# Low and high parts side by side in one 512-wide product, their sum formed by three engines

## The chip, the cores and the metric

One Trainium2 chip, of which the kernel uses one core. The metric is the device time of one execution in microseconds (us). TensorE does the matrix products, VectorE, ScalarE and GpSimd the rest, SyncE issues most DMAs. Each engine works through a queue of its own in order; semaphores hold one queue until another has got far enough.

## The reference, cut to what matters

Eight graphs of C = 1024 nodes with D = 256 features, hidden width 512. With H = (adj != 0) as 0/1 numbers, w the first row of adj, Dn = 1/(H w) and Be = 1/(column sums of H):

```
m   = Be * (H^T x)                 (S1)
z   = Dn * (H m)                   (S2)
h   = relu(z W1^T + b1)            (P, M)
q   = layernorm(h) W2^T            (Q)
m   = Be * (H^T q)                 (S3)
y   = Dn * (H m) + b2 + x          (S4)
x1  = layernorm(x + y)
out = layernorm(x1 + relu([x1, adj x1 / deg] WL^T))   (V, VM, L)
```

H holds only 0 and 1. x and m are f32 and are split into a high and a low f32r part, each of which is multiplied by H; the two products are summed.

## The kernel before, in words

Rows of 128 nodes are a tile, so a graph has NT = 8 tiles. For one graph TensorE runs the stages S2, P/M, Q, S3, S4, V/VM, L and then S1 of the next graph, with nothing between them. A bank of PSUM is 512 f32 columns wide; the table PRODUCT_BANKS gives the bank of each tile in each stage, and each stage waits for a bank until the tile that was in it before is emptied.

S1, S3 and S4 compute one output tile of 128x256 as 8 inner steps of two products each, one with the high and one with the low part (x_hi, x_lo, or m_hi, m_lo); both go to columns 0 to 255 of the bank. In S1 the high product is 258 wide: columns of ones behind x_hi count the column sums of H for Be. The helper tiled (L1077) runs S3, S4 and L: the first tiles of a stage (four in S3, two in S4) are filled step by step together, so the stage can start before its last input is there; the others follow one after the other, 8 steps each. Between the first three steps of S3 stand the last three tiles of Q. In front of tile 6 of S4 stand the transposes of tiles 0 and 1 of x1 (L1248), behind S4 the one of tile 2, and then V (L1267, L1268) and VM (L1274) take one tile of x1 at a time, with the transpose three tiles ahead. V waits until TX, the bank of the transpose, is emptied, which is take_x1 on ScalarE (L693, L695) and then x1_low on VectorE (L981).

Behind S1 and S3, ScalarE rounds Be times the bank into m_hi (L561) and VectorE takes the rest as m_lo (L790), which empties the bank. S4 and S2 want one tile of m a step. In S1, VectorE takes Be from the counted column (L832, L835), and between the tiles it builds the next rows of HT (L808).

Between the m_lo of S3, VectorE sums Dn of the next graph over 1024 columns with two inputs in SBUF (L758), in front of tiles 4, 5 and 7 and behind 7. Behind S4, VectorE adds Dn times the bank to the residual xres (L991), takes the moments of the row (L998, L1005), in tiles 2 to 6 builds a tile of H of the next graph (L747), and the reciprocal of the root (L774). ScalarE takes the root (L566), GpSimd two small shifts (L461, L463), ScalarE centres the rows (L687).

GpSimd's queue in a graph: z_cross (L470), the sums of squares (L477), x_lo (L481), the four operations on WL (L488, L493), the shifts with x1_cross (L500), the split of the next x (L432), the shifts of the last norm, and at the end the residual of the next graph: 8 doublings of x (L451) and 8 additions of b2 (L457). In the first graph the b2 additions stand before WL. ScalarE prepares WL_high and WL_cross (L679, L682) behind its last m_hi. SyncE loads x of the next graph when the residual is built, and adj of the next graph from the end of M on.

Of the kernel before, what the change touches and what calls it, by code (L numbers as in the profile page):

```python
# [42 lines left out]
H_EARLY = 5  # L43
X1_IN_H = 6
# [4 lines left out]
def graph_net(nc, x, adj, W1, b1, gamma, beta, W2, b2, WL, out):  # L49
# [80 lines left out]
    with ctx:  # L130
# [16 lines left out]
        x_hi, _, _ = place("x_hi", [P, NT, DP], F32R)  # L147
        x_lo, x_lo_at, _ = place("x_lo", [P, NT, D], F32R)
        m_hi, m_hi_at, _ = place("m_hi", [P, NT, D], F32R)
        m_lo, m_lo_at, _ = place("m_lo", [P, NT, D], F32R)  # L150
# [23 lines left out]
        hT, _, _ = place("hT", [P, NH, C], F32, m_hi_at)  # L174
# [15 lines left out]
        WL_high, _, nxt = place("WL_high", [P, ND, 2 * D], F32R, x_lo_at)  # L190
        WL_low, _, nxt = place("WL_low", [P, ND, 2 * D], F32R, nxt)
        assert nxt <= x_lo_at + 4 * NT * D
        WL_cross = [x_hi[:, 2 * d:2 * d + 2, 0:D] for d in range(ND)]
        x1_high = [x_hi[:, 2 * ND + n, 0:D] for n in range(X1_SLOTS)]
        x1_low, _, nxt = place("x1_low", [P, X1_SLOTS, D], F32R, H_at + 4 * C * X1_IN_H)
        x1_cross, _, nxt = place("x1_cross", [P, X1_SLOTS, D], F32R, nxt)
        assert nxt <= H_at + 4 * C * NT and 2 * ND + X1_SLOTS <= NT

        W1n, _, nxt = place("W1n", [P, NH, D], F32, m_hi_at)
# [6 lines left out]
        assert nxt <= m_lo_at + 4 * NT * D and m_lo_at == m_hi_at + 4 * NT * D  # L206
# [9 lines left out]
        zero_c = small[:, 23, 0:1]  # L216
        stats, _, _ = place("stats", [P, NT, 6], F32)
# [31 lines left out]
        be_done, rBe_ready, m_hi_done = (sem(n) for n in ("be_done", "rBe_ready", "m_hi_done"))  # L249
# [166 lines left out]
        def _(pool):  # L416
# [48 lines left out]
            def graph(b, more, first=False):  # L465
# [24 lines left out]
                for d in range(ND):  # L490
                    pool.wait_ge(WL_scaled, b * ND + d + 1)
                    pool.wait_ge(WL_low_done, b * ND + d + 1)
                    nc.gpsimd.tensor_tensor(WL_cross[d], WL_cross[d].bitcast(F32),  # L493
                                            WL_low[:, d, :].bitcast(F32).rearrange("p (a c) -> p a c", a=2),
# [30 lines left out]
        def _(act):  # L525
# [102 lines left out]
            def graph(b, more):  # L628
# [47 lines left out]
                for e in range(NT):  # L676
                    take_m_hi("S3", e, b, NT + e)
# [643 lines left out]
```

## Time and profile before

| | |
|---|---|
| median of 3 runs | 1051.67 us (1051.66 to 1051.96) |
| profiled execution | 1051.42 us, span 1049.6 us |
| TensorE busy | 1039.2 us of the span |
| VectorE busy | 776.7 us |
| ScalarE busy | 433.3 us |
| GpSimd busy | 435.6 us |

The span runs from the first to the last instruction of the core, the execution's own time is 1.8 us longer. TensorE's matmuls are pipelined: the duration of one in a row is longer than the distance from its start to the next one's start, and the pace is read from a stretch of many. An instruction of another engine that starts right behind one of its own does so some 0.05 to 0.1 us before the recorded end of the first.

### The profile page before, as it was taken

What the parts mean: (1) busy time and instruction counts of PE and PEld (TensorE: products, weight loads), DVE (VectorE), ACT (ScalarE), POOL (GpSimd) and SP (SyncE); (2) the same over time, 40 slices, a digit from 0 to 9 for tenths busy, and PEclk for the clock granted to TensorE, in tenths of its full rate; (3) what the DMA queues carried; (4) which work ended last, traced back from release to release, by engine and by line L of the source; (5) the groups of instructions that cost most, each with busy time, mean ns of one, the idle gap of its engine ahead of it and who ended that gap; (6) DMA issues with size and microseconds to landing.
All of it is one profiled execution on the core that took longest, in us unless ns stands there. A gap on an engine that the chain in (4) does not pass through costs nothing.

```text
span 1049.6 us, 19643 instructions
## 1 busy us (share of the span) xinstructions
PE 1039.2 (99%) x6241; PEld 933.2 (89%) x6241; DVE 776.7 (74%) x1848; ACT 433.3 (41%) x1029; POOL 435.6 (41%) x674
## 2 busy tenths in 40 slices
PE   8999999999999999999999999999999999999997
PEld 8889898898989989899898998989889898888986
DVE  6878786787867878677786778676786777867355
ACT  5553523445234442445325362254622536225350
POOL 0357416434254433534344353543525534265320
PEclk9999999999999999999999999999999999999999
DMA  8065431734227441274414644044440634400001
GB/s 296 3 138 117 98 90 34 152 92 103 64 59 156 96 98 31 60 160 100 90 30 87 133 100 100 20 114 106 100 100 20 142 78 100 110 11 1 2 1 40
DMA packets 72032, 90.01 MB, mean 86 GB/s; under 512 B 15544, under 2 KB 61248, under 8 KB 72000
## 3 DMA queue, kind: packets, MB, share of 16 engines
q1 hardware_dynamic: 63232, 85.49, 35.1%
q10 hardware_dynamic: 8768, 4.10, 1.7%
q8 instruction: 19, 0.31, 0.1%
q14 instruction: 13, 0.11, 0.0%
HBM read 81.14 MB, written 8.42 MB: 85 GB/s over the span
## 4 chain that ended last, share of the span: by engine, by line
PE 99%; DMA 0%; DVE 0%; issue 0%; ACT 0%; DVEq 0%
PE bank L1077 45%; PE bank L1107 12%; PE bank L1183 11%; PE bank L1231 11%; PE bank L1212 3%; PE bank L1219 3%; PE bank L1274 3%; PE bank L1267 3%; PE bank L1268 3%; PE bank L1211 3%; PE bank L1248 1%; PE bank L1068 1%; PE bank L1234 1%; DMA raw<-in_adj_dram 0%; PE bank L1172 0%; DVE xres L779 0%
## 5 line engine op out<-in xcount | busy, mean ns | idle before, releaser
L1077 PE MATMUL bank<-yv,adjT 128*128 128x257 f32 x1024 | 223.3, 379 | 0.0
L1077 PEld LDWEIGHTS bank<-yv,adjT 128*128 128x128 f32 x1024 | 193.6, 189 | 28.7
L566 ACT ACTIVATE small<-mv,small 128x1 f32<-128x1 f32 x192 | 56.0, 291 | 247.8 <-DVE mv L785 144.6
L1077 PE MATMUL bank<-x_hi,H 128*128 128x256 f32 x512 | 125.1, 286 | 0.0
L1231 PE MATMUL bank<-gW2T,hT 128*128 128x257 f32 x512 | 123.7, 385 | 0.0
L1107 PE MATMUL bank<-x_hi,H 128*128 128x258 f32 x512 | 123.6, 289 | 0.0
L1077 PE MATMUL bank<-x_lo,H 128*128 128x256 f32 x512 | 122.4, 280 | 0.0
L1077 PE MATMUL bank<-m_hi,HT 128*128 128x256 f32 x512 | 122.0, 281 | 0.0
L1077 PE MATMUL bank<-m_lo,HT 128*128 128x256 f32 x512 | 121.4, 279 | 0.0
L1107 PE MATMUL bank<-x_lo,H 128*128 128x256 f32 x512 | 119.2, 282 | 0.0
L561 ACT ACTIVATE m_hi<-bank,small 128x256 fp32r<-128x256 f32 x128 | 57.5, 474 | 136.2 <-DVE small L835 75.6
L1231 PEld LDWEIGHTS bank<-gW2T,hT 128*128 128x128 f32 x512 | 93.0, 190 | 11.5
L1183 PE MATMUL bank<-HT,m_lo 128*128 128x512 f32 x256 | 101.8, 398 | 0.0
L1183 PE MATMUL bank<-HT,m_hi 128*128 128x512 f32 x256 | 101.0, 395 | 0.0
L461 POOL TENSOR_TENSOR small<-mv,small 128x1 f32<-128x1 f32 x120 | 30.0, 250 | 170.0 <-DVE small L774 170.0
L1077 PEld LDWEIGHTS bank<-x_hi,H 128*128 128x128 f32 x512 | 96.8, 189 | 0.0
L1077 PEld LDWEIGHTS bank<-x_lo,H 128*128 128x128 f32 x512 | 96.3, 188 | 0.0
L1077 PEld LDWEIGHTS bank<-m_lo,HT 128*128 128x128 f32 x512 | 96.1, 188 | 0.0
L1077 PEld LDWEIGHTS bank<-m_hi,HT 128*128 128x128 f32 x512 | 96.1, 188 | 0.0
L790 DVE SCALAR_TENSOR_TENSOR m_lo<-bank,small,m_hi 128x256 fp32r<-128x256 f32 x128 | 59.2, 481 | 49.3 <-ACT m_hi L561 49.3
L1107 PEld LDWEIGHTS bank<-x_hi,H 128*128 128x128 f32 x512 | 93.9, 190 | 0.5 <-ACT bW_row L607 0.2
L1107 PEld LDWEIGHTS bank<-x_lo,H 128*128 128x128 f32 x512 | 93.1, 190 | 0.2
(132 smaller groups left out, 2203.1 us busy)
## 6 DMA issues: line engine op xcount, KB each, us to landing
raw<-in_adj_dram SPq DMA_DIRECT2D x112, 256.0 KB, 5.8
adjB<-in_adj_dram SPq DMA_DIRECT2D x224, 128.0 KB, 3.1
x_in<-in_x_dram SPq DMA_DIRECT2D x31, 256.0 KB, 6.1
out_dram<-xres SPq DMA_DIRECT2D x108, 64.0 KB, 1.6
raw<-in_adj_dram SPq DMA_DIRECT2D x8, 512.0 KB, 8.8
w_row<-in_adj_dram SPq DMA_DIRECT2D x8, 512.0 KB, 4.7
w_row<-rDn_row ACTq DMA_DIRECT2D x7, 512.0 KB, 9.0
out_dram<-xres SPq DMA_DIRECT2D x4, 256.0 KB, 2.1
```

The costliest lines, as they stand in the source:

```text
L561: nc.scalar.activation(m_hi[:, e, :], bank(stage, e)[:, 0:D], ACT.Identity, scale=rBe[:, e:e + 1])\
L566: nc.scalar.activation(std[:, i:i + 1], mv[:, which, i, 1:2], ACT.Sqrt, bias=eps_c)\
L790: empties_bank(nc.vector.scalar_tensor_tensor(out=m_lo[:, e, :], in0=bank(stage, e)[:, 0:D], scalar=rBe[:, e:e + 1], in1=m_hi[:, e, :].bit ...
L1077: last = mm(bank(stage, i)[:, 0:n_cols], lhsT, rhs, start=(k == 0 and part == 0), stop=(k == NT - 1 and part == parts - 1))
L1107: last = mm(*args, start=(c == 0 and n == 0), stop=(c == NT - 1 and n == 1))
L1183: last = mm(bank("S2", job)[:, :], m[:, k, d * P:(d + 1) * P], HT[:, k, ch * CH:(ch + 1) * CH], start=(k == 0 and n == 0), stop=(k == NT - ...
L1211: mm(bank("P", j)[:, :], W1_high[:, d, feats], z_high[:, d, nodes], start=(d == 0), stop=False)
L1212: last = mm(bank("P", j)[:, :], W1_low[:, d, feats], z_low[:, d, nodes], start=False, stop=(d == ND - 1))
L1219: last = mm(bank("M", j)[:, :], W1_cross[:, d, feats], z_cross[:, d, nodes], start=(d == 0), stop=(d == ND - 1))
L1231: mm(bank("Q", i)[:, 0:D + 1], hT[:, k, i * P:(i + 1) * P], gW2T[:, k, :], start=(k == 0), stop=(k == NH - 1))
L1267: mm(bank("V", i)[:, :], x1_high[n][:, part], WL_high[:, d, :], start=(d == 0), stop=False)
L1268: last = mm(bank("V", i)[:, :], x1_low[:, n, part], WL_low[:, d, :], start=False, stop=(d == ND - 1))
```

## The change

x_lo and x_hi lie side by side in one tensor x_both, m_hi and m_lo in m_both. S3, S4 and S1 of all graphs but the first multiply H or HT by both halves in one 512-wide product, so the bank holds the two halves' products beside each other and not their sum. The sum is formed outside TensorE:

- m (S1 of later graphs, and S3): ScalarE scales columns 0 to 255 into m_part, VectorE adds the scaled columns 256 to 511 (m_sum) and empties the bank, ScalarE rounds m_sum to m_hi, GpSimd takes m_lo. S2 and S4 wait for GpSimd (m_split).
- S4: ScalarE scales columns 256 to 511 into q_f32 (two slots), GpSimd adds that into the residual, and VectorE waits for it with its own addition of columns 0 to 255.
- The counted column is gone: VectorE sums each row of HT while it builds it (be_sum), and Be comes from that.
- GpSimd's WL operations move to behind its first four additions of S4; the b2 additions of the first graph move to between tiles 3 and 4 of m_lo. The doublings of the residual stand between the m_lo of S1.
- S1 of the first graph stays as it was.

```diff
-            def residual(b):
-
-                for t in range(NT):
-                    nc.gpsimd.tensor_tensor(xres[:, t, :], x_in[:, t, :], x_in[:, t, :], ALU.add).then_inc(xb_part, 1)
-                add_b2(b)
+            def double_x(t):
+                nc.gpsimd.tensor_tensor(xres[:, t, :], x_in[:, t, :], x_in[:, t, :], ALU.add).then_inc(xb_part, 1)
+
+            def take_m_lo(e, b, n):
+                pool.wait_ge(m_hi_done, b * (2 * NT) + (n + 1))
+                nc.gpsimd.tensor_tensor(m_lo[:, e, :], m_sum[:, e, :], m_hi[:, e, :].bitcast(F32), ALU.subtract).then_inc(m_split, 1)
...
-                if first:
-                    pool.wait_ge(bias_loaded, 16)
-                    add_b2(0)
-                for d in range(ND):
+                for e in range(NT):
+                    if first and e == S3_GROUP:
+                        pool.wait_ge(bias_loaded, 16)
+                        add_b2(0)
+                    take_m_lo(e, b, NT + e)
...
+                def add_y_part(i):
+                    pool.wait_ge(y_part_done, b * NT + i + 1)
+                    pool.wait_ge(xb_ready, b * NT + i + 1)
+                    nc.gpsimd.tensor_tensor(xres[:, i, :], xres[:, i, :], q_f32[:, i % 2, :], ALU.add)\
+                      .then_inc(y_part_added, 1)
...
-                for i in range(NT):
-                    if i in (NT - 3, NT - 2):
-                        take_x1_cross(i - (NT - 3))
-                    shift_of("1", 1, rstd_1, shift_1, mean_1_scaled, shift_1_done, i, b)
+                for i in range(NT + 1):
+                    if i < NT:
+                        add_y_part(i)
+                    if i < ND:
+                        take_WL_low(i)
+                    elif i < 2 * ND:
+                        take_WL_cross(i - ND)
+                    if i in (NT - 2, NT - 1):
+                        take_x1_cross(i - (NT - 2))
+                    if i > 0:
+                        shift_of("1", 1, rstd_1, shift_1, mean_1_scaled, shift_1_done, i - 1, b)
...
-                    pool.wait_ge(out_stored, b * OUT_B + OUT_0)
-                    residual(b + 1)
+                    for e in range(NT):
+                        take_m_lo(e, b + 1, e)
+                        if e == 1:
+                            pool.wait_ge(out_stored, b * OUT_B + OUT_0)
+                        if e > 0:
+                            double_x(e - 1)
+                    double_x(NT - 1)
+                    add_b2(b + 1)
...
+            def take_m_part(stage, e, b):
                 act.wait_ge(*full(stage, e, b))
                 act.wait_ge(rBe_ready, b * NT + (e + 1 if stage == "S1" else NT))
+                nc.scalar.activation(m_part[:, e, :], bank(stage, e)[:, 0:D], ACT.Identity,
+                                     scale=rBe[:, e:e + 1]).then_inc(m_part_done, 1)
+
+            def take_m_hi(stage, e, b):
+                act.wait_ge(*emptied(stage, e, b))
+                nc.scalar.activation(m_hi[:, e, :], m_sum[:, e, :], ACT.Copy).then_inc(m_hi_done, 1)
...
+                take_m_part("S3", 0, b)
                 for e in range(NT):
-                    take_m_hi("S3", e, b, NT + e)
+                    if e + 1 < S3_GROUP:
+                        take_m_part("S3", e + 1, b)
+                    elif e >= S3_GROUP:
+                        take_m_part("S3", e, b)
+                    take_m_hi("S3", e, b)
...
+                def take_y_part(i):
+                    act.wait_ge(*full("S4", i, b))
+                    if i == 0:
+                        act.wait_ge(rDn_ready, b + 1)
+                        act.wait_ge(q_split, b * NT + NT)
+                        if more:
+                            act.wait_ge(dn_ready, (b + 1) * NT + NT)
+                    elif i > 1:
+                        act.wait_ge(y_part_added, b * NT + i - 1)
+                    nc.scalar.activation(q_f32[:, i % 2, :], bank("S4", i)[:, D:2 * D], ACT.Identity,
+                                         scale=rDn[:, i:i + 1]).then_inc(y_part_done, 1)
+
+                take_y_part(0)
                 for i in range(NT):
+                    if i + 1 < NT:
+                        take_y_part(i + 1)
                     root("1", 1, std_1, i, b)
...
+            def add_m_parts(stage, e, b):
+                dve.wait_ge(m_part_done, b * (2 * NT) + (e - NT + 1 if stage == "S1" else e + 1))
+                empties_bank(nc.vector.scalar_tensor_tensor(
+                    out=m_sum[:, e, :], in0=bank(stage, e)[:, D:2 * D], scalar=rBe[:, e:e + 1],
+                    in1=m_part[:, e, :], op0=ALU.mult, op1=ALU.add), stage, e)
...
-                nc.vector.tensor_scalar(HT[:, k, :], adjT[:, k, :], 0.0, None, ALU.not_equal).then_inc(HT_ready, 1)
+                nc.vector.tensor_scalar(HT[:, k, :], adjT[:, k, :], 0.0, None, ALU.not_equal, ALU.add,
+                                        accum_out=be_sum[:, k:k + 1]).then_inc(HT_ready, 1)
...
                         dve.wait_ge(*full("S4", i, b))
+                        dve.wait_ge(y_part_added, b * NT + i + 1)
...
+            def s1_wide_step(e, c):
+                last = mm(bank("S1", e)[:, :], H_columns(c, e), x_both[:, c, 0:2 * D], start=(c == 0), stop=(c == NT - 1))
...
-                tiled("S3", b, D, lambda c: pe.wait_ge(q_split, b * NT + c + 1), 2,
-                      lambda c, e, part: (H_columns(c, e), (x_hi, x_lo)[part][:, c, 0:D]),
-                      group=4, behind_k=last_of_Q)
-                tiled("S4", b, D, lambda e: pe.wait_ge(*emptied("S3", e, b)), 2,
-                      lambda e, i, part: (HT[:, e, i * P:(i + 1) * P], (m_hi, m_lo)[part][:, e, :]),
+                tiled("S3", b, 2 * D, lambda c: pe.wait_ge(q_split, b * NT + c + 1), 1,
+                      lambda c, e, part: (H_columns(c, e), x_both[:, c, 0:2 * D]),
+                      group=S3_GROUP, behind_k=last_of_Q)
+                tiled("S4", b, 2 * D, lambda e: pe.wait_ge(m_split, b * (2 * NT) + (e + 1)), 1,
+                      lambda e, i, part: (HT[:, e, i * P:(i + 1) * P], m_both[:, e, :]),
                       before_last=lambda: (transpose_x1(0), transpose_x1(1)))
```

## Rows read from the trace of the kernel before

**Rows 1.** The page: busy time and instructions, granted clock in slices, last chain by engine.
```profile
PE 1039.2 (99%) x6241; PEld 933.2 (89%) x6241; DVE 776.7 (74%) x1848; ACT 433.3 (41%) x1029; POOL 435.6 (41%) x674
...
PEclk9999999999999999999999999999999999999999
...
PE 99%; DMA 0%; DVE 0%; issue 0%; ACT 0%; DVEq 0%
```

**Rows 2.** The chain in order of time, three pieces: start, us, line, count.
```profile
335.85 23.70 PE bank L1077 x200
...
404.06 15.14 PE bank L1107 x128
...
419.21 14.93 PE bank L1183 x64
```

**Rows 3.** Groups of instructions: count, busy us, mean ns, idle before.
```profile
L561 ACT ACTIVATE m_hi<-bank,small 128x256 fp32r<-128x256 f32 x128 | 57.5, 474 | 136.2 <-DVE small L835 75.6
...
L657 ACT ACTIVATE x_hi<-q_f 128x256 fp32r<-128x256 f32 x64 | 26.6, 416 | 28.2 <-DVE q_f L941 28.2
...
L481 POOL TENSOR_TENSOR x_lo<-q_f,x_hi 128x256 fp32r<-128x256 f32 x64 | 43.8, 690 | 58.4 <-ACT x_hi L657 58.4
```

**Rows 4.** Timelines of VectorE and ScalarE where S3 ends: start, us, what [idle before].
```profile
347.30 1.22 DVE L758 SCALAR_TENSOR_TENSOR unread<-raw,w_row 128x1024 bf16<-128x1024 f32 x1
...
348.78 0.48 DVE L790 SCALAR_TENSOR_TENSOR m_lo<-bank,small,m_hi 128x256 fp32r<-128x256 f32 x1 [0.26 <-ACT m_hi L561]
349.18 1.22 DVE L758 SCALAR_TENSOR_TENSOR unread<-raw,w_row 128x1024 bf16<-128x1024 f32 x1
...
348.27 0.47 ACT L561 ACTIVATE m_hi<-bank,small 128x256 fp32r<-128x256 f32 x1 [1.41 <-PE bank L1077]
```

**Rows 5.** Timeline of GpSimd during S4.
```profile
349.35 3.48 POOL L488 TENSOR_TENSOR WL_low<-WLT,WL_high 128x512 fp32r<-128x512 f32 x2 [10.82 <-ACT WL_high L679]
352.78 2.35 POOL L493 TENSOR_TENSOR x_hi<-x_hi,WL_low 128x512 fp32r<-128x512 f32 x2
...
358.88 0.19 POOL L461 TENSOR_TENSOR small<-mv,small 128x1 f32<-128x1 f32 x1 [1.24 <-DVE small L774]
359.14 0.19 POOL L463 TENSOR_TENSOR small<-small 128x1 f32<-128x1 f32 x1
...
363.03 0.59 POOL L463 TENSOR_TENSOR small<-small 128x1 f32<-128x1 f32 x1
```

**Rows 6.** Timeline of VectorE during S4.
```profile
357.46 0.72 DVE L747 TENSOR_SCALAR H<-raw 128x1024 fp32r<-128x1024 f32 x1
...
362.89 0.69 DVE L747 TENSOR_SCALAR H<-raw 128x1024 fp32r<-128x1024 f32 x1
...
363.90 0.47 DVE L991 SCALAR_TENSOR_TENSOR xres<-bank,small,xres 128x256 f32<-128x256 f32 x1
```

**Rows 7.** Timeline of TensorE: the first product of S4, and of V.
```profile
348.07 0.28 PE L1077 MATMUL bank<-m_hi,HT 128*128 128x256 f32 x1
...
363.73 0.48 PE L1267 MATMUL bank<-WL_high,x_hi 128*128 128x512 f32 x1
```

**Rows 8.** Timeline of GpSimd in S3 of the first graph.
```profile
82.62 9.60 POOL L457 TENSOR_TENSOR xres<-xres,b_row 128x256 f32<-128x256 f32 x8
```

**Rows 9.** Timelines of VectorE and GpSimd during S1.
```profile
411.98 0.68 DVE L808 TENSOR_SCALAR HT<-adjT 128x1024 fp32r<-128x1024 f32 x1
...
413.88 1.05 DVE L808 TENSOR_SCALAR HT<-adjT 128x1024 fp32r<-128x1024 f32 x1
...
423.38 0.49 DVE L790 SCALAR_TENSOR_TENSOR m_lo<-bank,small,m_hi 128x256 fp32r<-128x256 f32 x1 [0.54 <-ACT m_hi L561]
...
418.10 6.57 POOL L457 TENSOR_TENSOR xres<-xres,b_row 128x256 f32<-128x256 f32 x8
```

**Rows 10.** The chain in order of time at the start of the span.
```profile
6.48 2.57 PE bank L1107 x12
```

More of the change, by code:

```diff
@@ L43 @@
 H_EARLY = 5
+S3_GROUP = 4
 X1_IN_H = 6
@@ L146, in graph_net @@
         HT, HT_at, _ = place("HT", [P, NT, C], F32R)
[L147 to L150, printed above, removed]
+        x_both, _, _ = place("x_both", [P, NT, 2 * D + 2], F32R)
+        x_lo, x_hi = x_both[:, :, 0:D], x_both[:, :, D:D + DP]
+        m_both, m_at, m_end = place("m_both", [P, NT, 2 * D], F32R)
+        m_hi, m_lo = m_both[:, :, 0:D], m_both[:, :, D:2 * D]
+        m_f32, _, _ = place("m_f32", [P, NT, 2 * D], F32, m_at)
+        m_part, m_sum = m_f32[:, :, 0:D], m_f32[:, :, D:2 * D]
         x_in, _, _ = place("x_in", [P, NT, D], F32)
@@ L173, in graph_net @@
         ssum = (ssum_0, ssum_1)
-        hT, _, _ = place("hT", [P, NH, C], F32, m_hi_at)
+        hT, _, _ = place("hT", [P, NH, C], F32, m_at)
         assert nxt <= raw_at + 4 * NT * C
@@ L187, in graph_net @@
         unread, _, _ = place("unread", [P, C], BF16, q_at)
[L190 to L194, printed above, removed]
+        WL_high, WL_low, WL_cross = (x_both[:, n * ND:(n + 1) * ND, 0:2 * D] for n in range(3))
+        x1_high = [x_both[:, 3 * ND + n // 2, n % 2 * D:(n % 2 + 1) * D] for n in range(X1_SLOTS)]
         x1_low, _, nxt = place("x1_low", [P, X1_SLOTS, D], F32R, H_at + 4 * C * X1_IN_H)
         x1_cross, _, nxt = place("x1_cross", [P, X1_SLOTS, D], F32R, nxt)
-        assert nxt <= H_at + 4 * C * NT and 2 * ND + X1_SLOTS <= NT
-        W1n, _, nxt = place("W1n", [P, NH, D], F32, m_hi_at)
+        assert nxt <= H_at + 4 * C * NT and 3 * ND + X1_SLOTS // 2 <= NT
+        W1n, _, nxt = place("W1n", [P, NH, D], F32, m_at)
         W2n, _, nxt = place("W2n", [P, ND, DH], F32, nxt)
@@ L205, in graph_net @@
         mean_n, _, nxt = place("mean_n", [P, P], F32, nxt)
-        assert nxt <= m_lo_at + 4 * NT * D and m_lo_at == m_hi_at + 4 * NT * D
+        assert nxt <= m_end
         W2_mean, W2_sum = ssum_0[:, 0:D], ssum_0[:, D:2 * D]
@@ L216, in graph_net @@
         zero_c = small[:, 23, 0:1]
+        be_sum = col(21)
         stats, _, _ = place("stats", [P, NT, 6], F32)
@@ L733, in graph @@
                     for e in range(NT):
-                        take_m_hi("S1", e, b + 1, e)
+                        take_m_part("S1", e, b + 1)
+                        take_m_hi("S1", e, b + 1)
             over_graphs(act, graph)
@@ L1107, in s1_step @@
                     last = mm(*args, start=(c == 0 and n == 0), stop=(c == NT - 1 and n == 1))
+                if c == NT - 1:
+                    fills_bank(last, "S1", e)
+            def s1_wide_step(e, c):
+                last = mm(bank("S1", e)[:, :], H_columns(c, e), x_both[:, c, 0:2 * D], start=(c == 0), stop=(c == NT - 1))
                 if c == NT - 1:
@@ L1192, in graph @@
                     pe.wait_ge(HT_ready, b * NT + max(NT // NCH, k + 1))
-                    pe.wait_ge(*emptied("S1", k, b))
+                    if first:
+                        pe.wait_ge(*emptied("S1", k, b))
+                    else:
+                        pe.wait_ge(m_split, b * (2 * NT) + (k - NT + 1))
                     s2_step(0, k)
@@ L1273, in graph @@
                     for d in range(ND):
-                        last = mm(bank("VM", i)[:, :], x1_cross[:, n, d * P:(d + 1) * P], WL_cross[d],
+                        last = mm(bank("VM", i)[:, :], x1_cross[:, n, d * P:(d + 1) * P], WL_cross[:, d, :],
                                   start=(d == 0), stop=(d == ND - 1))
```

66 lines of the change are left out of this document (34 added, 32 removed).

## The prediction

> **What bounds the kernel now.** I read the page's busy shares first [rows 1]: TensorE is busy for 99% of the span, its granted clock is at the upper level (2.4 GHz) in every slice, and the chain that ended last is TensorE for 99%. So only two things can move the time: the pace of TensorE's products, and holes opened in its row of work. Then the chain in order of time [rows 2]. 200 products of 256 columns (S3 and S4) take 23.70 us, 0.1185 us each. 128 of S1 (258 and 256 columns) take 15.14 us, 0.1183 each. The 64 products of S2, also f32r but 512 columns wide, take 14.93 us, 0.2333 each. A wide product thus costs almost exactly what two narrow ones do; the weight load, one for each product in both forms, is hidden in both. Third, the timelines of the other engines at the two seams that the change touches, S3 to S4 and S4 to V, in one graph of the middle [rows 4 to 7].
>
> **Term 1, TensorE's pace.** A pair becomes one product. S3 and S4: 2 x 0.1185 - 0.2333 = 0.0037 us a pair, 64 pairs a stage, 0.24 us a stage, 16 stages: 3.8 us. S1 of the seven later graphs: 2 x 0.1183 - 0.2333 = 0.0033, x 64 x 7 = 1.5 us. In all 5.2 us less; from below the bound is 0 (the row of S2 may not carry over), from above 5.2.
> By the Trainium skill (TensorE: Matmul & The Clock Gate, the section on start-to-start spacing) a sustained stream of weight load and matmul has about 131 ns for 512 columns and 81 ns for 128. By that, a pair of halves would cost well more than one whole product, and the change would save tens of us. This trace has 233.3 ns for 512 columns [rows 2], and the measurement decides.
>
> **Term 2, the seam from S3 to S4.** Before, a tile of m is one ScalarE and one VectorE step: the m_hi of tile 7 starts at 348.27, its m_lo at 348.78, and is there at 349.26 [rows 4]. S4 starts at 348.07 [rows 7] and wants tile 7 seven steps of 0.47 us later, at 351.3, so two us are spare. Now four steps stand in a row: ScalarE's part (0.47), VectorE's sum (0.48), ScalarE's rounding from SBUF (0.42, as x_hi), GpSimd's difference (0.69, as x_lo) [rows 3]. VectorE's long sums for Dn stand between them, and they and GpSimd exclude each other: the first WL_low overlaps the Dn sum of 349.18, and the pair takes 3.48 us [rows 4, 5] where the next two take 2.35. Walked queue by queue: sums of the first four tiles end at 343.6 instead of 342.7; Dn4, tile 4, Dn5, tile 5 follow; tile 6 is summed at 348.3; Dn6 runs to 349.9; tile 7 is summed to 350.4, rounded to 350.8, and its difference waits behind Dn7 (about 350.6 to 351.8) and ends at 352.5. Wanted at 351.2: TensorE waits 1.3 us. Without the exclusion nothing would be late here: bounds 0 and 1.3, I take 1.3 since the WL_low row shows the exclusion in this very place.
>
> **Term 3, the seam from S4 to V, the main one.** Before, GpSimd does the four WL operations (349.35 to 355.13) while S4 runs, and then only small shifts of 0.27 + 0.14 us a tile [rows 5]. Afterwards its queue holds for each tile of S4 an addition into the residual, and VectorE's own addition waits for it; the WL operations stand between the first four, and each turn also waits for VectorE's H tile when the two meet (the shift at 363.03 takes 0.59 instead of 0.19 under the H tile of 362.89 [rows 5, 6]). S4's first tiles are full at 353.0 (term 2), ScalarE's part ends at 353.5, and GpSimd goes:
> - turn 0: add 0.65, WL 1.2: 1.85 us
> - turn 1: add, WL, shift 0.4: 2.3 us
> - turns 2 and 3: add, WL, shift, and 0.6 behind an H tile: 2.85 us each
> - turns 4 to 6: add, shift, 0.6 behind H, and the round trip to VectorE for the reciprocal that the shift needs (0.7): about 2.4 us each.
> TensorE wants 1.87 us a tile. The additions of tiles 5 and 7 end at 366.5 and 371.3; VectorE's final sum of tile 7 stood at 363.90 [rows 6]. What hangs on it: the transposes in front of tile 6 need row tile 1 centred (shift 1 ends at 360.6, centring at 361.3, wanted at 360.4 to 360.6): 0.6 us. V0 needs x1_low(0), which VectorE issues behind its work on tile 5: 368.3 to 368.65. So the third transpose and V0 start at 368.7 and 368.9, where V0 started at 363.73 [rows 7]. V1 needs x1_low(1) behind tile 6, V2 the one behind tile 7: 371.3 and 373.5, 2.4 and 2.2 us apart instead of 1.6; ScalarE brings V3 at 375.55. From there the old pace holds. V ends 6.8 us later than before. This includes terms 1 (S3, S4) and 2. The same walk made of the kernel before gives 363.95 for V0 and 364.28 for the sum of tile 7, so its own error is some 0.3 us. A full exclusion counts a little too much, as GpSimd holds the way for less than its whole operation: I take 6.5 us a graph, for the six graphs 1 to 6. With no exclusion at all the walk gives 3.6.
>
> **Term 4, the two other graphs.** The last graph has no Dn sums and no H tiles: 2.3 us. The first has the eight b2 additions in GpSimd's queue between tiles 3 and 4 of m_lo; before, they took 9.60 us beside Dn [rows 8] and nobody waited. Now S4's fifth step stands behind them: 5.9 us instead of 1.3, in all about 11 us for this graph (5 without exclusion).
>
> **Term 5, S1 to S2.** VectorE now makes be_sum with its HT rows, and the operation may lose its 0.68 us and take the 1.2 us of a Dn sum with its accumulator read. The old m_lo of tile 7 was done at 423.86 [rows 9], S2 wants it at 425.5. With 0.68 (or the 1.05 of a row that met GpSimd [rows 9]) GpSimd's last difference ends at 423.2; with 1.3 and no exclusion at 425.7, 0.2 late; with 1.3 and exclusion S2 loses 2.3 us. I take 0, since 0.68 is the row of the same operation without the sum [rows 9]; seven graphs could add 16 us. The residual, ending 5 us later (429.9 for 424.67 [rows 9]), still lies before the products that need z_cross (435). The next graph's x_in load waits for it, but its adj load waits for the end of M at 445 anyway, as before. SyncE's and ScalarE's DMA issues move with TensorE and are not late for anybody.
>
> **Sum.** 6 x 6.5 + 11 + 2.3 - 1.5 (S1) = 50.8; against the profiled execution's 1051.42 us this is 1102, and that execution is 0.25 us under the median of 1051.67, which is nothing here. I say 1100.
>
> **Rivals.**
> - A, less exclusion: GpSimd and VectorE disturb each other less in the new order than the rows of the old one say. Speaks for it: most H tiles of the old stage took their own 0.72 us [rows 6], with small shifts beside them. 6 x 3.6 + 5 + 2.3 - 1.5 = 27: 1079. Chance 0.17.
> - B, the clock: holes of 3.5 us in front of V, and of 5.9 in the first graph, let the granted clock fall to 1.2 GHz. At the start of this trace 12 of S1's narrow products took 2.57 us, 0.214 each [rows 10] instead of 0.118, right after TensorE had stood still. If each of 8 graphs paid a stretch like the 4.5 to 9.5 us of that start, 2.5 us each: 1120. The Trainium skill (TensorE: Matmul & The Clock Gate, rules for kernel authors) says that an idle gap between bursts sends the array back to half rate; no hole of that size is in this trace after the start, so no row here tells. Against: the transposes and first tiles break the hole up. Chance 0.06.
> - C, the faster side: the additions hide. It decides whether GpSimd's turn stays under 1.87 us a tile. It would if a narrow addition took half of what x_lo's row says (0.35 for 0.69) and if VectorE's queue never waited. Then only term 1 is left: 1051.4 - 5.2 = 1046. Against: 8 additions, 4 WL, 8 shifts and 2 x1_cross are 5.3 + 4.8 + 3.3 + 1.3 = 14.7 us of GpSimd alone in a stage of 11.3 us. Chance 0.09.
> - D, both sides cancel within 0.2%, which is what a measurement of this kernel can tell from none (2.1 us): 0.04.
> - E, be_sum makes the HT rows slow (term 5), on top of the forecast: up to 1116. Chance 0.08.
> The forecast keeps 0.56.
>
> **Range.** From 1068 (between A and D) to 1118 (E and most of B). Slower by over 0.2%: 0.56 + 0.17 + 0.06 + 0.08 = 0.87; faster 0.09; same 0.04.
>
> **What would show it.** TensorE's busy share falls to about 95%; the waits show TensorE's transposes of x1 (the helper before V) waiting for VectorE's x_low, some 3.5 us a graph, and a wait of S4's step 7 for GpSimd's m_lo of about 1.3 us. GpSimd is busy 8 + 8 + 8 more operations a graph. A wide product starts each 0.233 us. V0 of the third graph starts some 5 us later after S3's start than before. I am wrong in the main term if S4's eight sums of VectorE still come each 1.9 us; wrong in term 1 if wide products come faster than 0.233.

## The result, and the profile after

| | before | after |
|---|---|---|
| median | 1051.68 us (1051.66 to 1051.96) | 1110.23 us (1109.31 to 1111.06) |
| span of the profiled execution | 1049.6 us | 1108.3 us |
| ratio | | 1.0556, interval 1.0538 to 1.0574 |

The forecast was 1100 us in a range of 1068 to 1118, with 0.87 on slower. The change costs 58.6 us.

The page of the changed kernel: busy times and instructions of each engine, the granted clock in 40 slices, the last chain by engine, and one group (busy, mean ns, idle time before it and its releaser).

```profile
PE 1053.2 (95%) x4769; PEld 867.1 (78%) x4769; DVE 808.5 (73%) x1904; ACT 499.3 (45%) x1213; POOL 574.5 (52%) x858
...
PEclk9998899999999999999999999999999999999999
...
PE 53%; POOL 25%; issue 13%; DVE 6%; ACT 1%; POOLq 0%; DMA 0%; DVEq 0%; ACTq 0%
...
L1053 DVE SCALAR_TENSOR_TENSOR xres<-bank,small,xres 128x256 f32<-128x256 f32 x64 | 31.0, 484 | 69.0 <-POOL xres L507 69.0
```

TensorE issues 1472 products fewer than in [rows 1], its busy share falls from 99 to 95%, and the last chain is no longer its own: GpSimd has a quarter of it. GpSimd's additions into the residual (L507) are what VectorE's sums behind S4 wait for, 69.0 us in 64 waits. The page shows dips of the clock in slices 4 and 5 only; a slice is 27.7 us long, and shorter dips in other graphs vanish in it (they are shown with term 4 below).

Where the time went shows in the chain: the first product of L (128 products) in each graph. First the changed kernel, then the kernel before.

```profile
133.70 27.76 PE bank L1139 x128
...
403.41 27.76 PE bank L1139 x128
...
1074.66 27.76 PE bank L1139 x128
```

```profile
120.45 27.75 PE bank L1077 x128
...
376.31 27.75 PE bank L1077 x128
```

The first graph costs 13.25 us (133.70 - 120.45). From the first L to the seventh (942.97, and 888.06 before) it is 809.27 us for 767.61, so six graphs cost 41.7, 6.9 each. The last costs 3.7 (131.69 from L to L for 128.02). That makes 58.6, and the last 0.1 to the spans' difference of 58.7 lies behind the last L.

Within a graph: S3 of the third one starts at 347.75, its L at 403.41, 55.66 us, where the kernel before took 49.33 (326.98 to 376.31, the L of the second fence). So 6.3 us come in S3, S4 and V together, and the other 0.6 between L and the next S3, although S1 got 0.38 us shorter (14.95 us from its first product to the first of S2, 15.33 before). The waits of TensorE's weight loads in that graph, with the idle time before each and who ended it:

```profile
372.48 7.65 PEld L1139 LDWEIGHTS bank<-m_both,HT 128*128 128x128 f32 x34 [0.95 <-POOL m_both L457]
...
388.82 0.20 PEld L1317 LDWEIGHTS bank<-ident,xres 128*128 128x128 f32 x2 [3.62 <-DVE x_low L1042]
391.18 0.20 PEld L1317 LDWEIGHTS bank<-ident,xres 128*128 128x128 f32 x2 [0.88 <-DVE x_low L1042]
...
462.64 0.30 PEld L1288 LDWEIGHTS bank<-z_cross,W_cross 128*128 128x128 f32 x2 [1.15 <-issue]
```

The first is S4's step 7, the next two the third transpose of x1 and the one behind V0 (behind V1 it is 0.96), the last stands in front of M. In these rows a load stands ahead of its product: the product's own idle time at these places is 0.53, 3.20, 0.45, 0.53 (behind V1) and 0.74 us. Two more waits of products belong to the list: 0.75 us in front of the second transpose of x1, for ScalarE's centred row, and 0.23 behind V2. The six in S4 and V make 5.7 us. The stretch lost more, 6.3 us and the 0.5 that the pace of S3 and S4 gave back, as the work behind a wait takes longer too: from the third transpose to the next are 2.36 us, 0.45 of them waiting and 1.91 not, and it is 1.60 from one transpose to the next where nothing waits (397.26 to 398.86).

GpSimd in S4 of that graph (only the additions into the residual and one small shift between them):

```profile
373.79 0.74 POOL L507 TENSOR_TENSOR xres<-xres,q_f 128x256 f32<-128x256 f32 x1 [1.36 <-ACT q_f L748]
...
375.74 0.74 POOL L507 TENSOR_TENSOR xres<-xres,q_f 128x256 f32<-128x256 f32 x1
...
377.90 0.74 POOL L507 TENSOR_TENSOR xres<-xres,q_f 128x256 f32<-128x256 f32 x1
...
379.84 0.64 POOL L466 TENSOR_TENSOR small<-mv,small 128x1 f32<-128x1 f32 x1
...
380.70 0.72 POOL L507 TENSOR_TENSOR xres<-xres,q_f 128x256 f32<-128x256 f32 x1
...
383.49 0.75 POOL L507 TENSOR_TENSOR xres<-xres,q_f 128x256 f32<-128x256 f32 x1
385.38 1.21 POOL L507 TENSOR_TENSOR xres<-xres,q_f 128x256 f32<-128x256 f32 x1
387.90 1.05 POOL L507 TENSOR_TENSOR xres<-xres,q_f 128x256 f32<-128x256 f32 x1
```

```profile
379.72 0.71 DVE L804 TENSOR_SCALAR H<-raw 128x1024 fp32r<-128x1024 f32 x1
```

From addition to addition GpSimd takes 1.95, 2.16, 2.80 and 2.79 us, and the last three end 2.36 apart. TensorE fills a tile in 1.87. The small shift of 379.84 takes 0.64 us in place of 0.19 because it lies under VectorE's H tile of 379.72 (second fence), and an addition that meets an H tile takes 1.05 or 1.21 in place of 0.74.

### The profile page after: what moved, and what is told of

Read it like the earlier page. It is cut to its first block, busy times and chain, and to the rows that moved or that the text cites. A ratio compares the mean times of both kernels' runs of the same rounds, so it can differ in the third digit from the quotient of the medians.

```text
span 1108.3 us, 17525 instructions
## 1 busy us (share of the span) xinstructions
PE 1053.2 (95%) x4769; PEld 867.1 (78%) x4769; DVE 808.5 (73%) x1904; ACT 499.3 (45%) x1213; POOL 574.5 (52%) x858
## 4 chain that ended last, share of the span: by engine, by line
PE 53%; POOL 25%; issue 13%; DVE 6%; ACT 1%; POOLq 0%; DMA 0%; DVEq 0%; ACTq 0%
PE bank L1139 23%; PE bank L1300 10%; POOL m_both L457 7%; POOL xres L507 4%; POOL xres L462 4%; PE bank L1288 3%; POOL xres L453 3%; PE bank L1280 2%; PE bank L1281 2%; PE bank L1336 2%; PE bank L1337 2%; PE bank L1343 2%; POOL x_both L501 2%; POOL x_both L495 2%; POOL z_cross L475 2%
## 5 line engine op out<-in xcount | busy, mean ns | idle before, releaser
L457 POOL TENSOR_TENSOR m_both<-m_f,m_both 128x256 fp32r<-128x256 f32 x120 | 109.0, 921 | 90.1 <-ACT m_both L598 89.9
L1139 PE MATMUL bank<-m_both,HT 128*128 128x512 f32 x512 | 125.0, 400 | 8.6 <-POOL m_both L457 8.6
L1139 PE MATMUL bank<-x_both,H 128*128 128x512 f32 x512 | 126.7, 399 | 0.0
L1249 PE MATMUL bank<-HT,m_both 128*128 128x512 f32 x512 | 122.3, 397 | 0.0
L1139 PEld LDWEIGHTS bank<-m_both,HT 128*128 128x128 f32 x512 | 96.6, 191 | 32.4 <-POOL m_both L457 11.7
L1249 PEld LDWEIGHTS bank<-HT,m_both 128*128 128x128 f32 x512 | 95.6, 188 | 25.1 <-issue 2.7
L1139 PEld LDWEIGHTS bank<-x_both,H 128*128 128x128 f32 x512 | 94.3, 189 | 19.4
L1173 PE MATMUL bank<-x_both,H 128*128 128x512 f32 x448 | 105.9, 396 | 0.0
L1173 PEld LDWEIGHTS bank<-x_both,H 128*128 128x128 f32 x448 | 84.5, 189 | 18.7
L482 POOL TENSOR_TENSOR ssum<-ssum,hpre 128x512 f32<-128x512 f32 x48 | 64.0, 1333 | 49.1 <-DVE hpre L990 48.3
L728 ACT ACTIVATE xres<-xres,small 128x256 f32<-128x256 f32 x120 | 70.9, 591 | 6.6 <-POOL small L468 6.5
L815 DVE SCALAR_TENSOR_TENSOR unread<-raw,w_row 128x1024 bf16<-128x1024 f32 x50 | 64.6, 1292 | 9.5 <-POOL x_both L486 9.1
```

Of the source, the lines that this page charges most:

```text
L457: nc.gpsimd.tensor_tensor(m_lo[:, e, :], m_sum[:, e, :], m_hi[:, e, :].bitcast(F32), ALU.subtract).then_inc(m_split, 1)
L482: nc.gpsimd.tensor_tensor(ssum[j // NH][:, :], ssum[j // NH][:, :], hpre[:, j % T_SLOTS, :], ALU.add)\
L728: nc.scalar.activation(xres[:, i, :], xres[:, i, :], ACT.Identity, scale=rstd[:, i:i + 1], bias=shift[:, i:i + 1]).then_inc(normed[norm], 1)
L815: nc.vector.scalar_tensor_tensor(out=into[:, :], in0=raw[:, c, :], scalar=0.0, in1=w_row[:, :], op0=ALU.not_equal, op1=ALU.mult, accum_out ...
L1139: last = mm(bank(stage, i)[:, 0:n_cols], lhsT, rhs, start=(k == 0 and part == 0), stop=(k == NT - 1 and part == parts - 1))
L1173: last = mm(bank("S1", e)[:, :], H_columns(c, e), x_both[:, c, 0:2 * D], start=(c == 0), stop=(c == NT - 1))
```

## The experiments

Each kernel is the changed one with the edit shown, but for the combined ones, which say what they start from.

### S4 narrow again

```diff
-                tiled("S4", b, 2 * D, lambda e: pe.wait_ge(m_split, b * (2 * NT) + (e + 1)), 1,
-                      lambda e, i, part: (HT[:, e, i * P:(i + 1) * P], m_both[:, e, :]),
+                tiled("S4", b, D, lambda e: pe.wait_ge(m_split, b * (2 * NT) + (e + 1)), 2,
+                      lambda e, i, part: (HT[:, e, i * P:(i + 1) * P], (m_hi, m_lo)[part][:, e, :]),
```

together with the removal of take_y_part, add_y_part and VectorE's wait for y_part_added.

> S4 alone goes back to two 256-wide products a step into the same columns; ScalarE's and GpSimd's share of S4's sum is gone, all else stays as changed. Theory (GpSimd's turn in S4 is the main loss): the hole in front of V goes and V comes at its old distance, about 5.5 us less in each of graphs 1 to 6 and in the first; what stays is the hole at S4's step 7 (1 us), the one in front of M (1 us), and the b2 hole of the first graph. 1110 becomes about 1071 us. Rival (the wide products or the seam from S3 to S4 carry the loss): above 1095 us.

Measured: 1065.18 us (1064.65 to 1066.21), ratio 1.013 (1.0113 to 1.0146), 6 us below what was expected. The split of S4's sum over three engines is 45 of the 58.6 us. L stands 128.9 us from L, 1.0 above the kernel before, and the first L is at 127.77, 7.3 late. Two of the waits that are left, of the loads over the whole trace (us, count, longest):

```profile
PEld bank L1133 <- POOL m_both L457: 9.5, 7, 5.5
...
PEld bank L1311 <- DVE x_low L1037: 2.2, 8, 0.3
```

L1133 is S4 (5.5 us of it in the first graph, 0.66 in each of six), L1311 the transposes, whose waits have all but gone. The product in front of M still waits as before (6.8 us of its loads in seven graphs).

### S4 wide, but its low half left out of the sum

This kernel makes S4 512 wide and leaves columns 256 to 511 of S4 out of the residual: a part of the computation is missing.

```diff
-                        add_y_part(i)
...
-                        dve.wait_ge(y_part_added, b * NT + i + 1)
```

and the same for take_y_part.

> S4 stays 512 wide, but the low half of its bank is not added to the residual (left out of the computation): ScalarE's y part and GpSimd's addition are gone. Theory: the wide product costs nothing, only its sum does: within 3 us of s4_narrow and if anything below it (8 x 0.24 = 2 us for the pace), so about 1069 us. Rival (wide products into a full bank are themselves slower or disturb others): over 5 us above s4_narrow.

Measured once: 1062.86 us, L 128.63 us from L. This is 2.3 us under the narrow S4, near the 8 x 0.24 of the pace; from L to L it is 0.25 less (128.88 and 128.63). Wide products themselves hurt nothing here; only forming the sum does.

### H tiles out of S4

```diff
-H_EARLY = 5
+H_EARLY = 0
```

VectorE then builds no H tile between its sums of S4, but all of them behind.

> The changed kernel with H_EARLY = 0: VectorE builds all eight H tiles of the next graph behind V, none beside S4. Theory (GpSimd's additions and shifts stand still under each H tile, which makes its turns 2.8 and 2.4 us instead of 2.2 and 1.8): the turns shorten by some 0.6 us where an H tile stood, V comes about 3 us earlier in seven graphs, and 1110 becomes about 1088 us. Rival (GpSimd's turn is its own work alone): turns stay and the time stays within 4 us, or rises as the H tiles come late for L and S1.

Measured: 1114.58 us (1113.34 to 1115.83), ratio 1.0599 (1.0583 to 1.0616): no gain, but 4.4 us more than the changed kernel, where the theory had 22 less. The turns did shorten. GpSimd in S4 of the third graph:

```profile
378.71 0.74 POOL L507 TENSOR_TENSOR xres<-xres,q_f 128x256 f32<-128x256 f32 x1
379.41 1.30 POOL L501 TENSOR_TENSOR x_both<-x_both 128x512 fp32r<-128x512 f32 x1
380.67 0.19 POOL L466 TENSOR_TENSOR small<-mv,small 128x1 f32<-128x1 f32 x1
...
385.32 0.74 POOL L507 TENSOR_TENSOR xres<-xres,q_f 128x256 f32<-128x256 f32 x1
```

The shift is 0.19 again, and the turns that start at 378.71 and 381.08 take 2.37 and 2.35 us (2.80 and 2.79 with the H tiles). The next two, without WL, end 1.89 and 1.96 apart in place of 2.36, near the 1.87 that TensorE wants. The wait in front of the third transpose falls from 3.62 to 2.18 us, and from S3's first product to L's it is 53.3 us in the six middle graphs (53.29 to 53.45) in place of 55.5: 2.2 us of the 6.3 are the H tiles' doing. But from L to the next S3 it is 81.6 to 83.0 us in place of 79.3, which takes more than that back: the H tiles push S1's sums back, and S2 now waits for m:

```profile
PEld bank L1249 <- POOL m_both L457: 13.6, 12, 1.2
```

So the part of my theory on the exclusion holds in the place it speaks of, and the total I drew from it was wrong: I had counted the H tiles' new place as free, against which the rival had warned.

### VectorE adds the low half itself

```diff
-                        add_y_part(i)
...
+                        dve.wait_ge(y_part_done, b * NT + i + 1)
+                        nc.vector.tensor_tensor(xres[:, i, :], xres[:, i, :], q_f32[:, i % 2, :], ALU.add)\
+                          .then_inc(y_part_added, 1)
                         dve.wait_ge(y_part_added, b * NT + i + 1)
```

> The changed kernel, but VectorE and not GpSimd adds ScalarE's part of S4 to the residual; the wide products and ScalarE's step stay. Theory (it is GpSimd's queue that holds S4 up): VectorE's turn grows from 1.7 to about 2.1 us against 1.87 of TensorE, so some 2 us a graph stay of the 6: about 1080 us. Rival (the round trip by ScalarE and the order of its queue hold S4 up, whoever adds): above 1100 us.

Measured: 1111.3 us (1111.11 to 1111.42), ratio 1.0564 (1.0548 to 1.058). Expected was a gain of 30 us; there is none. VectorE in S4 and one of GpSimd's operations on WL:

```profile
375.84 0.43 DVE L1051 TENSOR_TENSOR xres<-xres,q_f 128x256 f32<-128x256 f32 x1
...
377.43 1.49 DVE L1051 TENSOR_TENSOR xres<-xres,q_f 128x256 f32<-128x256 f32 x1
...
383.76 0.39 DVE L1051 TENSOR_TENSOR xres<-xres,q_f 128x256 f32<-128x256 f32 x1
```

```profile
377.34 1.30 POOL L501 TENSOR_TENSOR x_both<-x_both 128x512 fp32r<-128x512 f32 x1
```

VectorE's addition, which has both inputs in SBUF, takes 0.39 to 0.43 us alone and 1.49 beside a WL operation: the blocked side changed, not the block. The additions that met WL start 3.21 and 3.12 us before the next one. And the addition alone, with the sum, the moments and an H tile, is 2.10 us a tile (from 383.76 to the next one at 385.86), still over 1.87. The rival, ScalarE's round trip, had the time right (above 1100), but it is not what these rows show: the parts that the additions of 377.43 and 380.64 take were ready at 376.61 and 378.71, and VectorE's row has no idle time between 375.84 and 392. In this order the sum is too much for either queue; VectorE's addition with the H tiles or WL elsewhere was not run.

### The b2 additions split around z_cross

```diff
-                    add_b2(b + 1)
+                    add_b2(b + 1, range(NT // 2))
...
+                    if ch == 0 and not first:
+                        add_b2(b, range(NT // 2, NT))
```

the second behind the first two z_cross of S2.

> In the changed kernel, GpSimd's additions of b2 for tiles 4 to 7 move from the end of S1 to behind the first two z_cross of the next graph. Theory (the hole in front of M comes from VectorE's z_low and GpSimd's z_cross standing behind and beside those additions): the hole of 1.15 us goes in seven graphs, 1110 becomes about 1103 us. Rival (it comes from the slower HT rows alone): no change within 1 us.

Measured: 1105.02 us (1104.59 to 1105.34), ratio 1.0505 (1.0487 to 1.0522), 5.2 us less than the changed kernel. In S2 of the changed kernel VectorE's z_low, which also has both inputs in SBUF, stood beside the b2 additions:

```profile
453.32 5.67 POOL L462 TENSOR_TENSOR xres<-xres,b_row 128x256 f32<-128x256 f32 x8
...
459.62 2.91 POOL L475 TENSOR_TENSOR z_cross<-z_high,z_low 128x512 fp32r<-128x512 f32 x2 [0.63 <-DVE z_low L973]
```

```profile
455.83 4.30 DVE L973 SCALAR_TENSOR_TENSOR z_low<-z_f,z_cross 128x512 fp32r<-128x512 f32 x2 [0.62 <-ACT z_cross L670]
```

With the split, the same two take

```profile
453.14 1.78 DVE L975 SCALAR_TENSOR_TENSOR z_low<-z_f,z_cross 128x512 fp32r<-128x512 f32 x2 [0.62 <-ACT z_cross L672]
```

and no product waits for z_cross any more. From L to the next S3 it is now 78.5 us in place of 79.3, 0.8 less in each of seven graphs, a little more than the 0.74 that the product in front of M had waited. That 5.2 / 7 is 0.74 too is chance: the first graph got 1.0 us shorter, and the fourth and the seventh took 0.8 us longer from S3 to L than the others (56.4 and 56.2 for 55.6). In those two the granted clock stayed low for some 6 to 7 us in V; this is the fourth:

```profile
519.00:526.50 7.50, 6.04 (x17) 4.72 (x18) 6.12 (x22) 5.30 (x16) 5.58 (x13) 0.54 0.72 200
```

(Stretch, length, busy time and count of TensorE, its weight loads, VectorE, ScalarE and GpSimd, granted clock as a share of 2.4 GHz, DMA share, GB/s.)

### The first graph's b2 additions moved out of m_lo

On top of the last one:

```diff
+                if first:
+                    pool.wait_ge(bias_loaded, 16)
+                    add_b2(0, range(NT // 2))
...
-                    if ch == 0 and not first:
+                    if ch == 0:
...
-                    if first and e == S3_GROUP:
-                        pool.wait_ge(bias_loaded, 16)
-                        add_b2(0)
```

> As b2_split, and in the first graph the b2 additions stand before and between its z_cross too, no longer between tiles 3 and 4 of m_lo. Theory (the first graph's extra 6 us are the hole of 5.75 us at S4's step 4 and the lower clock behind it): 6 to 8 us below b2_split, about 1096 us, and a mean granted clock back above 0.995. Rival (clock and hole hang on the later hole in front of V): under 3 us and the clock stays at 0.986.

Measured: 1100.41 us (1100.32 to 1100.66), ratio 1.0462 (1.0444 to 1.0479), another 4.6 us, under the 6 to 8 expected; the first L starts at 129.04 in place of 132.72. S4's start in the first graph, first as changed, then with this edit:

```profile
99.07 0.50 PEld L1139 LDWEIGHTS bank<-m_both,HT 128*128 128x128 f32 x2 [5.75 <-POOL m_both L457]
```

```profile
98.08 7.64 PEld L1141 LDWEIGHTS bank<-m_both,HT 128*128 128x128 f32 x34 [0.97 <-POOL m_both L457]
```

The hole of 5.75 us is the 0.95 of every graph now; half of the additions still stood in the way of z_cross, where two new holes of up to 1.70 us gave a part back. The mean granted clock was to be above 0.995 again and is 0.989: the first graph has no dip any more, but V of five later graphs has one, that of the seventh graph long enough for the page to show it. Theory and rival each had a part of it.

### The last Dn sum behind m_lo

On S4 narrow. Expected was that the hole at S4's step 7, where GpSimd's last m_lo stands beside VectorE's last Dn sum, goes when the sum is held back.

```diff
+                if more:
+                    dve.wait_ge(m_split, b * (2 * NT) + NT)
                 next_Dn((NT - 1,), unread)
```

> s4_narrow, with VectorE's last Dn sum held back until GpSimd has taken the last m_lo of S3. Theory (the hole at S4's step 7 is m_lo standing behind that sum in the shared way): the hole of 1.0 us falls to some 0.3 us in seven graphs, 1065 becomes about 1060 us. Rival (the four steps in a row are too long by themselves): no change, or worse by the sum that now runs into S4.

Measured: 1066.39 us (1066.08 to 1066.88), ratio 1.0138 (1.0122 to 1.0153), 1.2 more than S4 narrow. Two waits answer:

```profile
PEld bank L1135 <- POOL m_both L457: 4.5, 1, 4.5
...
PEld bank L1313 <- DVE x_low L1039: 12.7, 28, 0.7
```

The hole is gone in all graphs but the first, and the sum, now in S4, makes x_low late. From L to L it is 129.40 us in place of 128.88, 0.5 more a graph, and the first graph is 1.1 us shorter, so the total hides most of the loss. Cause right, cure wrong.

### Combined: S1 and S3 wide, S4 narrow

Four kernels, all with S4 narrow, the b2 additions split, those of the first graph between the x_lo of Q, and ScalarE's m_part of S1 one tile ahead of its m_hi. The first also holds the last Dn sum back, the second doesn't. The third leaves tile 7 of S3 as two 256-wide products, and its m_hi and m_lo as one ScalarE and one VectorE step:

```diff
+                    if stage == "S3" and i == NT - 1:
+                        for part in range(2):
+                            last = mm(bank(stage, i)[:, 0:D], H_columns(k, i), (x_hi, x_lo)[part][:, k, 0:D],
+                                      start=(k == 0 and part == 0), stop=(k == NT - 1 and part == 1))
...
```

The fourth is the third with the four WL operations in one piece behind m_lo.

> S1 and S3 wide, S4 narrow, with every hole treated: the Dn sum held back as in s4n_dn7; b2 of tiles 4 to 7 behind the first two z_cross; b2 of the first graph between the x_lo of Q; in S1, ScalarE's part of tile e + 1 ahead of the rounding of tile e. Theory (with no hole left only the pace remains, 0.21 us a graph in S1 and 0.24 in S3): 1051.7 - 1.5 - 1.9 = 1048.3 us, up to 1052 if some of the hole at step 7 stays. Rival (wide products bring a loss of their own that the waits do not show): above 1054 us.

> S1 of later graphs and S3 wide, S4 narrow, b2 additions split as before, Dn7 back in its old place behind S3's sums. Against the version with Dn7 held (1055.6) the wait of S4's step 7 for GpSimd's m_lo comes back (0.95 us in each of 7 graphs, 6.7 us) and the waits for x_low in S4 (13.7 us over 29 loads, but the loads run ahead, so only a part is TensorE's) go. In the pair without the b2 edits holding Dn7 cost 1.2 us. Theory (the holes and the 3.4 us of pace are all there is): 1054.4. Rival (the x_low waits were real time): 1048.6.

> As s13_plain, but tile 7 of S3 stays two 256-wide products into one bank, and its m_hi and m_lo are one ScalarE and one VectorE step as in the kernel before. Theory (the hole at S4's step 7 comes from the four-step chain over three engines behind Dn6 and Dn7): the hole goes, at a price of 8 x 0.0037 us a graph. 1054.4 - 6.7 + 0.2 = 1048, which is 0.35% under the kernel before. Rival (tile 6 is then the late one: its difference on GpSimd runs beside Dn6): the hole moves to step 6 with up to 0.9 us, 1053 to 1054.

> As s13_tile7, with GpSimd's four WL operations back in one piece behind the last m_lo, as in the kernel before, and not between its shifts. Theory: the waits for x_low that S4 narrow showed (2.2 us in 8) go, 0 to 2 us less than s13_tile7, 1046 to 1048. Rival: WL_low beside Dn7 makes Dn7 long and the first sums of S4 late: 1 to 3 us more.

| kernel | median us | ratio to before | interval | L to L, us |
|---|---|---|---|---|
| Dn sum held | 1055.6 | 1.0036 | 1.0022 to 1.0049 | 128.54 |
| Dn sum in place | 1052.5 | 1.0005 | 0.9996 to 1.0014 | 128.06 |
| tile 7 of S3 narrow | 1047.47 | 0.9958 | 0.9944 to 0.9971 | 127.40 |
| and WL in one piece | 1051.16 | 0.9991 | 0.9982 to 1.0 | 127.83 |

The third beats the kernel before by 0.42%. The theory had said 1048 for it. Two of its lines: every wait of TensorE's loads for x_low, and the wide S1.

```profile
PEld bank L1335 <- DVE x_low L1054: 2.2, 8, 0.3
```

```profile
403.04 14.78 PE bank L1191 x64
```

No wait for m is left at all, and one L follows the other after 127.40 us in place of 127.93. The 0.53 are the pace: 15.14 - 14.78 = 0.36 in S1, and 7/8 of 0.24 = 0.21 in S3, together 0.57. Holding the Dn sum back cost 3.1 us (1055.6 against 1052.5), not the 1.2 of the other pair; from L to L it is the same 0.5 us in both pairs, and only the first graphs differ. The second kernel lies between what theory (1054.4) and rival (1048.6) gave it. The fourth kernel loses 3.7 us to the third, on the rival's side, with the waits for x_low back:

```profile
PEld bank L1336 <- DVE x_low L1055: 9.1, 23, 0.7
```

But the rival's mechanism is not the cause: the last Dn sum takes 1.36 us in both kernels, with WL_low beside it in both. What differs in the rows is GpSimd's first shift, behind four WL operations in the one and behind two in the other. In the fourth kernel:

```profile
350.48 3.34 POOL L499 TENSOR_TENSOR x_both<-WLT,x_both 128x512 fp32r<-128x512 f32 x2
353.78 2.54 POOL L505 TENSOR_TENSOR x_both<-x_both 128x512 fp32r<-128x512 f32 x2
356.28 0.64 POOL L466 TENSOR_TENSOR small<-mv,small 128x1 f32<-128x1 f32 x1
```

and in the third:

```profile
349.19 3.33 POOL L499 TENSOR_TENSOR x_both<-WLT,x_both 128x512 fp32r<-128x512 f32 x2
352.65 0.19 POOL L466 TENSOR_TENSOR small<-mv,small 128x1 f32<-128x1 f32 x1
```

The first shift starts 5.8 us behind the start of WL_low in the one, 3.5 in the other. VectorE's first H tile differs too: it meets the fourth WL operation there and takes 1.48 us, and 0.81 in the third kernel. Which of the two makes x_low late was not taken apart. So WL among the shifts, one move of the change, is a gain once S4 is narrow.

## Why the prediction was right, and where it was not

**The direction and the main term (3) held.** I had GpSimd's turns at 1.85, 2.3, 2.85, 2.85 and then 2.4; they are 1.95, 2.16, 2.80, 2.79 and 2.36. V0 was to start 5.2 us late and V to be slower for two tiles; V0 of the third graph started 4.6 us late (41.36 us behind S3's start for 36.75), V lost 1.7 more, and the stretch from S3 to L grew by 6.3 us, where I took 6.5. S4 narrow shows that this is the change's main cost, 45 us over eight graphs. The reason I gave, GpSimd and VectorE excluding each other at the H tiles, is shown where the H tiles were taken away: the same stretch then grew by 4.2 us. My figure without any exclusion was 3.6; no run shows it, since GpSimd still met the Dn sums there.

The Trainium skill (SBUF — State Buffer, Who interferes with whom) says that a VectorE operation with two SBUF inputs, or one in a mode that uses both ports, and a GpSimd operation that reads SBUF lock each other out for a whole instruction. The rows agree: 0.43 became 1.49 beside 1.30, and a shift of 0.19 became 0.64 under an H tile of 0.71. They come out slightly under a lock for the whole instruction, as term 3 had assumed: the addition started 0.09 us into the 1.30, so 1.21 + 0.43 = 1.64 would have been full.

**Term 1, the pace, held** for S3 and S4: 0.25 us from L to L for S4. In S1 the change gave more than the 0.21 of the sum: 14.78 for 15.14, 0.36 a graph.

**Term 2 was too large.** I had 1.3 us at S4's step 7. The load waited 0.95, the product 0.53. The mechanism is the one I named: GpSimd's last m_lo takes 1.33 us beside the Dn sum of 1.35, in place of 0.74 alone, and with the Dn sum held back, or tile 7 off that chain, the wait is gone.

```profile
371.10 1.33 POOL L457 TENSOR_TENSOR m_both<-m_f,m_both 128x256 fp32r<-128x256 f32 x1 [0.34 <-ACT m_both L598]
...
370.49 1.35 DVE L815 SCALAR_TENSOR_TENSOR unread<-raw,w_row 128x1024 bf16<-128x1024 f32 x1
```

**Term 4, the first graph, was 2.25 us too small.** The hole of 5.9 us was there, as 5.75. What I left out is that the clock fell behind it. In windows of the changed kernel (columns as above):

```profile
98.00:105.00 7.00, 5.92 (x16) 4.66 (x17) 0.91 (x2) 0.84 (x2) 4.85 (x7) 0.59 0.77 150
...
118.00:122.00 4.00, 3.75 (x11) 3.06 (x12) 3.29 (x11) 2.94 (x9) 3.57 (x8) 0.50 0.84 222
...
254.00:257.00 3.00, 3.00 (x9) 2.31 (x10) 2.49 (x8) 2.33 (x8) 2.76 (x6) 0.50 0.66 197
...
359.00:404.00 45.00, 39.32 (x175) 30.51 (x174) 31.57 (x78) 26.83 (x69) 30.17 (x45) 1.00 0.30 75
```

The first stretch, at 0.59 of full speed, lies behind the hole of 5.75 us. The 40 products behind that hole took 11.5 us (99.08 to 110.61), where 40 at the upper level of 2.4 GHz, 0.233 each [rows 2], are 9.3: 2.2 us. The second stretch is part of a longer one at the lower level behind the third transpose, 118 to 124 us, and cost another 0.9 (15.3 us from that transpose to L, 14.4 in the third graph). Against these 3.1 us the first graph lacks the 0.75 in front of its second transpose.

The third stretch lies behind the third transpose of the second graph. That transpose waits 3.2 us in each of the first seven graphs. So what rival B feared did happen, and not in one graph alone: the granted clock fell to the lower level of 1.2 GHz in V of six of these seven graphs (0.59, 0.52, 0.56 and 0.50 of full speed at 523 to 526, 660 to 663, 794 to 797 and 930 to 933 us), and stayed at 1.00 only in the third. But it cost next to nothing there. From S3 to L the third graph takes 55.49 us, and the second and the fourth to seventh, with the dip, 55.52 to 55.56. In the third graph V's next products wait for x_low (0.45 and 0.53 us), in the second they don't: the slower work fills what was waiting time. So rival B's mechanism was right and its price, 2.5 us for each graph, was not. Why the third graph was spared the rows do not tell.

**The last graph was too cheap:** from S3 to L it took 3.2 us more than before (52.36 for 49.15), where I had 2.3. No run takes this apart; the kernel without H tiles in S4 has the same 52.36 in its last graph.

**Term 5 is the step that failed.** I put it at nothing: the row of HT keeps its 0.68 us, and the residual, ending later, still lies before the products that need z_cross. The first was wrong, and from the second nothing followed. VectorE and GpSimd in S1 of the changed kernel:

```profile
439.84 1.21 DVE L870 TENSOR_SCALAR_CACHE_REDUCE HT<-adjT 128x1024 fp32r<-128x1024 f32 x1
440.97 0.08 DVE L870 DVE_READ_ACCUMULATOR HT<-adjT 128x1 f32 x1
...
440.45 0.74 POOL L457 TENSOR_TENSOR m_both<-m_f,m_both 128x256 fp32r<-128x256 f32 x1 [1.22 <-ACT m_both L598]
```

An operation that also sums its row is a different instruction with an extra read, 1.29 us for 0.68 [rows 9]. It is the slow case that I named in rival E, but without E's loss: all 56 rows together are 67.7 us, none under 1.199 or over 1.220, with GpSimd's m_lo of 0.74 beside many of them, so neither held the other up, and S2's loads wait at most 0.3 us. The Trainium skill (SBUF — State Buffer, Who interferes with whom) states just this: the form of tensor_scalar that also writes out its accumulator is left out of the two-port modes. I had not weighed that sentence; it takes the gain of the second port away and the exclusion with it.

What I did lose here I had looked for in the wrong place. The residual does end before the products that need z_cross, but its eight additions stand beside VectorE's z_low, which comes before z_cross: z_low took 4.30 us for two in place of 1.78, z_cross follows, and M waits 0.74 us. The split shows it: 0.8 us from L to S3 in each of seven graphs. The slow rows of HT probably have a share in this, which no run measured: VectorE's turns in S1 became 1.94 us against TensorE's 1.87, and the residual ended 13.2 us behind S2's first product, where the walk with rows of 0.68 had 10.9 (429.9 - 419.04) and z_low starts at 10.1.

So the 7.8 us between my sum of 50.8 and the 58.6 measured are: 2.25 in the first graph, 5.5 between L and S3 (0.57 more in each of seven graphs, where the sum had 0.21 less), 0.9 in the last graph and 0.1 behind it, less 1.0 because term 3 was too large by 0.16 in each of six. Saying 1100 for a sum of 1102 made the gap to 1110.2 larger by two.

## What to carry to other kernels

A sum that TensorE forms for nothing in its bank costs three queues when it is taken apart: before trading it for a few ns of pace (here 4 a pair), add up each helper's turn for a tile, with what it is locked out by, and compare it with TensorE's pace for that tile. Here the sums of S1 and S3 could be afforded once the places where the engines met were cleared, and that of S4, with a turn of 1.9 to 2.8 us against 1.87, could not. Where a long chain ends a stage, the last tile alone can keep the short form: one narrow tile of eight turned a draw (1052.5) into a gain of 0.42% (1047.47).

## What the runs showed that I had not expected

- A row operation with a sum took 1.21 us plus 0.08 for the read and was not slowed by GpSimd; the same without the sum took 0.68, or 1.05 where it met GpSimd [rows 9].
- Moving the residual's addition from GpSimd to VectorE changed nothing (1111.3 against 1110.2): the lock between the two follows the operation.
- The granted clock fell behind most waits of 3.2 us, and the graphs with such a dip took no longer than the one without, since the work behind it was waiting for VectorE. A mean clock of 0.986 is no measure of time lost.
- Idle time before a weight load overstates what TensorE loses, and that before its product understates it a little: 0.95 against 0.53 at step 7, and 1.15 against 0.74 in front of M, where taking the wait away gave 0.8 a graph.
